# Attention values of two heads made at once with tokens standing, in a fused attention and feed-forward kernel on one core

## The reference

```python
q = (x @ wq).reshape(B, S, 32, 128)
k = (x @ wk).reshape(B, S, 8, 128)
v = (x @ wv).reshape(B, S, 8, 128)
q, k = _rope(q, pos), _rope(k, pos)
allowed = (j <= i) & (j > i - 128)
attn = softmax(where(allowed, q @ k.T * 128**-0.5, neg))
s = (attn @ v).reshape(B, S, 32 * 128) @ wo
g = (silu(xn @ gate) * (xn @ up)) @ down
```

## Time and profile before

| | |
|---|---|
| median of 3 runs (lowest to highest) | 873.48 us (872.38 to 873.61) |
| the profiled execution | 873.48 us |
| its span on the core | 871.0 us |
| mean granted TensorE clock | 0.999 of full |
| instructions | 14447 |
| HBM read, written | 63.41 MB, 8.39 MB |

### The profile page before, as it was taken

One profiled execution on the slowest core, in us unless ns is written; L12 is line 12 of the kernel. 1 busy time (PEld: TensorE's weight loads), 2 busy tenths in 40 slices (PEclk: granted clock), 3 DMA queues, 4 the chain that ended last, 5 costly groups with the idle time before them and its releaser, 6 DMA issues.

```text
span 871.0 us, 14447 instructions
## 1 busy us (share of the span) xinstructions
PE 861.2 (99%) x4340; PEld 725.6 (83%) x4340; DVE 674.5 (77%) x1264; ACT 493.5 (57%) x1322; POOL 577.2 (66%) x500
## 2 busy tenths in 40 slices
PE   8999999999999999999999999999999999999997
PEld 7888888888888888888888888888888888888886
DVE  8877777877686877877776877778665888989876
ACT  5766565655656566656556555665564444444443
POOL 4665566666675776667666757764446887888865
PEclk9999999999999999999999999999999999999999
DMA  8111110131003012100311020116374564655542
GB/s 263 38 49 37 36 39 25 26 97 36 25 14 106 24 36 90 30 24 24 96 36 36 24 85 24 36 48 159 85 212 120 144 179 132 177 150 167 161 133 96
DMA packets 94851, 72.25 MB, mean 83 GB/s; under 512 B 4192, under 2 KB 80480, under 8 KB 94816
## 3 DMA queue, kind: packets, MB, share of 16 engines
q1 hardware_dynamic: 94096, 70.70, 27.6%
q10 hardware_dynamic: 720, 1.11, 0.4%
HBM read 63.41 MB, written 8.39 MB: 82 GB/s over the span
## 4 chain that ended last, share of the span: by engine, by line
PE 91%; DVE 5%; ACT 2%; DMA 1%; POOL 1%; issue 1%; SPq 0%; DVEq 0%
PE ps L38 29%; PE ps L39 29%; PE ps L40 29%; PE ps L1099 3%; PE ps L1079 1%; ACT probs L1242 1%; DMA work<-L_attn_wv 1%; DVE ps L1507 1%; DMA y<-L_attn_x 0%; DVE work L1503 0%; DVE work L1502 0%; DVE work L1509 0%; POOL w_lo L983 0%; POOL pt_lo L1373 0%; DVE xt_lo L1471 0%
## 5 line engine op out<-in xcount | busy, mean ns | idle before, releaser
L38 PE MATMUL ps<-xt_hi,w_lo 128*128 128x512 f32 x412 | 164.5, 399 | 0.4 <-POOL w_lo L209 0.4
L39 PE MATMUL ps<-xt_lo,w_hi 128*128 128x512 f32 x412 | 161.5, 392 | 0.0
L40 PE MATMUL ps<-xt_hi,w_hi 128*128 128x512 f32 x412 | 160.7, 390 | 0.0
L1373 POOL TENSOR_TENSOR pt_lo<-kept,pt_hi 128x512 fp32r<-128x512 f32 x112 | 142.8, 1293 | 24.9 <-ACT pt_hi L1253 24.6
L1368 POOL TENSOR_TENSOR q_lo<-work,q_hi 128x512 fp32r<-128x512 f32 x63 | 81.3, 1292 | 90.9 <-ACT q_hi L1225 90.9
L1242 ACT ACTIVATE probs<-ps,neg_max 128x128 f32<-128x128 f32 x256 | 90.7, 366 | 42.8 <-DVE neg_max L1527 42.8
L1253 ACT ACTIVATE pt_hi<-kept 128x512 fp32r<-128x512 f32 x112 | 69.2, 633 | 65.6 <-DVE kept L1540 65.6
L38 PE MATMUL ps<-wo_hi,o_lo 128*128 (+1 forms) x256 | 99.8, 390 | 0.1
L40 PE MATMUL ps<-wo_hi,o_hi 128*128 (+1 forms) x256 | 99.6, 389 | 0.0
L39 PE MATMUL ps<-wo_lo,o_hi 128*128 (+1 forms) x256 | 99.6, 389 | 0.0
L40 PEld LDWEIGHTS ps<-xt_hi,w_hi 128*128 128x128 f32 x412 | 77.5, 188 | 17.4
(11 more groups left out here) (174 smaller groups left out, 2234.7 us busy)
## 6 DMA issues: line engine op xcount, KB each, us to landing
work<-L_attn_wq SPq DMA_DIRECT2D x32, 256.0 KB, 2.8
work<-L_attn_wo SPq DMA_DIRECT2D x32, 256.0 KB, 2.7
work<-L_ffn_gate_w SPq DMA_DIRECT2D x14, 256.0 KB, 3.7
work<-L_ffn_gate_z SPq DMA_DIRECT2D x14, 256.0 KB, 4.6
work<-L_ffn_gate_s SPq DMA_DIRECT2D x14, 256.0 KB, 5.8
work<-L_ffn_up_w SPq DMA_DIRECT2D x14, 256.0 KB, 2.9
work<-L_ffn_up_z SPq DMA_DIRECT2D x14, 256.0 KB, 4.0
work<-L_ffn_up_s SPq DMA_DIRECT2D x14, 256.0 KB, 4.5
```

The source lines that it names most:

```text
L38: pe.matmul(out, stat[1], mov[0], start=first, stop=False, skip_group_check=grown)
L39: pe.matmul(out, stat[0], mov[1], start=False, stop=False, skip_group_check=grown)
L40: return pe.matmul(out, stat[0], mov[0], start=False, stop=last, skip_group_check=grown)
L1373: pool.tensor_tensor(pt_lo[:, w, :], kept[:, w, :], pt_hi[:, w, :].bitcast(F32), ALU.subtract).then_inc(pt_split, 1)
```

## The change

Values are made for two heads at once, in the heads with even number (par = 0): the transposed input of 128 tokens stands and the value weights of heads g and g + 1 (256 columns) move. A product (piece 5 or 6) makes two of a batch's four token tiles, 2 x 4 k x 3 = 24 matmuls; the result has tokens on the partitions. v_t, `drain_v`, `turn_v` and their semaphore go, and `hi_of_v` and `lo_of_v` work on half the tokens of two heads each. The heads are issued in pairs: 0 and 1, a loop over pairs (2, 3) and (4, 5), then 6 and 7. An even head has 11 weight pieces, an odd one 9, so `SPLIT_AT` has a table for each. While a unit (g, b) is worked off, seven products are made ahead if par equals b (`with_values`), two of them values; otherwise five are made, and of the last query (`HALVED = 4`) k = 0, 1 are made behind j = 1 and k = 2, 3 at j = 2.

```diff
         def over_heads(eng, body):
-            body(0, False)
-            with eng.Fori(1, NKV - 1) as g:
-                body(g, False)
-            body(NKV - 1, True)
+            for g in range(2):
+                body(g, g, False)
+            with eng.Fori(1, NKV // 2 - 1) as pair:
+                body(pair * 2, 0, False)
+                body(pair * 2 + 1, 1, False)
+            body(NKV - 2, 0, False)
+            body(NKV - 1, 1, True)
...
+        SPLIT_AT = (
+            {(0, 0): (0,), (0, 1): (1, 2), (0, 2): (3,), (0, 3): (4, 5), (1, 0): (6,), (1, 1): (7, 8), (1, 2): (9,), (1, 3): (10,)},
+            {(0, 0): (0,), (0, 1): (1,), (0, 2): (2,), (0, 3): (3, 4), (1, 1): (5,), (1, 2): (6, 7), (1, 3): (8,)})
...
+        HALVED = 4
+
+        def with_values(par, b):
+
+            return par == b
+
+        def before(g, par, b, j):
+            if first_unit(g, b):
+                return (2, 4, 5)[j]
+            return (1, 3, 5)[j] if with_values(par, b) else (1, 3, HALVED)[j]
+
+        def after(g, par, b, j):
+            if first_unit(g, b):
+                return (3, None, 6)[j]
+            return (2, 4, 6)[j] if with_values(par, b) else (2, HALVED, None)[j]
+
+        def left(g, par, b, j):
+
+            if first_unit(g, b):
+                return (1, 3, None)[j]
+            return (None, 2, 4)[j] if with_values(par, b) else (None, 2, None)[j]
...
+                if k >= V_:
+
+                    for t in range(2):
+                        tile = slice(b * SEQ + (2 * (k - V_) + t) * P, b * SEQ + (2 * (k - V_) + t + 1) * P)
+                        for c in ks:
+                            last = three_passes(pe, out[:, t * 2 * P:(t + 1) * 2 * P], (xt_hi[:, c, tile], xt_lo[:, c, tile]),
+                                                [values_weights(w)[:, c, :] for w in (w_hi, w_lo)], c == 0, c == KT - 1)
...
                         turn_probs(n)
-                        if ahead and j == QB - 1:
-                            turn_v(un, bn)
                         if j < QB - 1:
                             scores(n + 1, unit, b, j + 1)
                         elif ahead:
                             scores(n + 1, un, bn, 0)
                         if ahead and j < QB - 1:
-                            project(gn, un, bn, before(g, b, j))
+                            first = before(g, par, b, j)
+
+                            project(gn, pn, bn, first, range(2, KT) if j == 2 and first == HALVED else range(KT))
...
-                        if ahead and j < QB - 1 and after(g, b, j):
-                            project(gn, un, bn, after(g, b, j))
+                        if ahead and j < QB - 1 and after(g, par, b, j):
+                            second = after(g, par, b, j)
+                            project(gn, pn, bn, second, range(2) if j == 1 and second == HALVED and not with_values(par, b) else range(KT))
```

On DVE (ACT and POOL in the same way, with the high and low part of the row) the step's middle becomes:

```diff
-                        if ahead and j < QB - 1 and left(g, b, j):
-                            rope(un, bn, left(g, b, j), n + 1 if early else None)
-                        if ahead and j == QB - 1:
-                            lo_of_v(un, bn)
+                        if ahead and j < QB - 1 and left(g, par, b, j):
+                            rope(gn, pn, bn, left(g, par, b, j), n + 1 if early else None)
+                        if ahead and j == QB - 1 and with_values(par, b):
+                            lo_of_v(gn, bn, 1)
                         if more and not early:
                             invert(n + 1)
-                        if ahead and j < 2:
-                            rope(un, bn, before(g, b, j))
-                        if ahead and j == 2:
-                            drain_v(un, bn)
+                        if ahead and roped_beside(g, par, b, j):
+                            rope(gn, pn, bn, before(g, par, b, j))
+                        if ahead and j == 2 and with_values(par, b):
+                            lo_of_v(gn, bn, 0)
```

More of the change, by code:

```diff
@@ L255, in step @@
     def step(self, pool, g, k):
-        x = lambda part, row, hf: self.tokens(part, g, row, hf)
+        whole = lambda row, hf: (self.tokens(0, g, row, hf), self.tokens(1, g, row, hf), ALU.add)
         t1, t2, t3, t4 = (self.row(i) for i in range(4))
-        first, second = self.more[:, 0, :, :], self.more[:, 1, :, :]
         to, a, b, op, needs = (
[L262 to L271, removed]
+            (t1, *whole(0, 1), None),
+            (t2, *whole(0, 0), None),
+            (t1, t1, t2, ALU.subtract, 2),
+            (t3, *whole(1, 1), None),
+            (t4, *whole(0, 1), None),
+            (t3, t3, t4, ALU.subtract, 5),
+            (t2, *whole(1, 1), None),
+            (t2, t2, t1, ALU.subtract, 7),
+            (t4, *whole(1, 0), None),
+            (t4, t4, t2, ALU.subtract, 9))[k]
         if needs is not None:
-            pool.wait_ge(self.sh.sum_step, g * self.STEPS + (needs - self.STEPS))
+            pool.wait_ge(self.sh.sum_step, g * self.STEPS + (needs - 2 * self.STEPS))
         pool.tensor_tensor(to, a, b, op).then_inc(self.sh.sum_step, 1)
@@ L521, in add_gate2 @@
         wait(dve, self.seven_silu, 2 * blk - 1)
-        dve.tensor_tensor(self.gate2[:, :], self.bank(self.C), self.copies[:, 2, :], ALU.add).then_inc(self.added, 1)
+        dve.tensor_tensor(self.copies[:, 2, :], self.bank(self.C), self.copies[:, 2, :], ALU.add).then_inc(self.added, 1)
     def add_up2(self, dve, blk):
@@ L530, in silu_gate2 @@
         wait(act, self.seven_mid, 2 * blk)
-        act.activation(self.sh.tables[:, 1, :], self.gate2[:, :], ACT.Silu).then_inc(self.seven_silu, 1)
+        act.activation(self.sh.tables[:, 1, :], self.copies[:, 2, :], ACT.Silu).then_inc(self.seven_silu, 1)
     def silu_gate1(self, act, blk):
@@ L699, in high_parts @@
                 wait(act, gated, TT - 4 + i)
[L700 removed]
+                act.activation(gate_of(TT - 1 + i)[:, half], acc(TT - 1, half), ACT.Silu).then_inc(gate_done, 1)
         def low_parts(pool):
@@ L1337, in body @@
                         behind = first_unit(g, b) and j == 1
-                        if ahead and j < 2 and not behind:
-                            hi_of_roped(un, bn, before(g, b, j))
+                        if ahead and roped_beside(g, par, b, j) and not behind:
+                            hi_of_roped(gn, pn, bn, before(g, par, b, j))
+                        if ahead and j == 2 and with_values(par, b):
+                            hi_of_v(gn, bn, 0)
                         if not last and j == QB - 1:
-                            hi_of_roped(unit + 2, b, 0)
+                            hi_of_roped(g + 1, 1 - par, b, 0)
                         if last:
```

352 lines of the change are left out of this document (175 added, 177 removed).

## The result

The changed kernel takes 892.15 us (median of 4 runs, 891.08 to 892.41) against 873.53 before: a ratio of 1.0218 with a 95% interval of 1.0205 to 1.0231. The forecast was 887.2 us, its range 881 to 893. Direction and range held; the sum is 5 us short, and the missing part has one main cause, a fall of TensorE's granted clock that the sum had left out.

A forecast was written before the change was run, and what follows sets the result against it. TensorE was taken as the bound, busy 99% of the span with 91% of the chain. Terms -7.0 + 2.1 + 20.0 - 0.5 - 0.9 = +13.7 on 873.5 gave 887.2 us, range 881 to 893.

The forecast's parts named there:

- Removed work, -7.0: TensorE, all 16 units: the four transposes of v_t go, 0.44 us a unit, 7.0 us less.
- Added matmuls, +2.1: TensorE value products: 384 matmuls of 256 columns at 0.119 us for 192 of 512 at 0.227, +2.1 us.
- The wait: TensorE before the scores at j = 3 waits for row 4's low part: 2.5 us in 8 five-product units, +20.0.
- the 0.2 for a late DVE: Part of each wait: lost cover in the step before makes DVE late by up to 0.27 us, 0.2 taken.
- Other covers at nothing: Other steps of five- and seven-product units: cover still holds, no further TensorE wait opens, costed at 0.
- a sign of being wrong: Profile after: the forecast is wrong if TensorE's idle time in the loop ends by something other than POOL q_lo.
- The ends, -0.5 and -0.9: First unit's extra product beyond the sum: -0.5 us (-1 to +2); last head's shorter waits: -0.9 (-1.2 to 0).
- The clock: TensorE's granted clock: full in the forecast; the rival, chance 0.05, loses 2.4 us at each of eight waits, 906 us.
- Rival 2: Second wait, at the weighing of j = 2 for pt_lo: up to 1.3 us in 4 units, 892 us, chance 0.12.
- Rival 1: No wait before the scores at j = 3, row 4's low part being ready: 867.2 us, chance 0.13.

The follow-up runs named there:

- Run 8: Kernel before without the values' four transposes and the copy into v_t (wrong attention values), first feed-forward product's wait kept as before: 869.20 us, ratio 0.9953.
- Run 7: Kernel before with each value product issued as 24 matmuls of 256 columns instead of 12 of 512: 874.38 us, ratio 1.0016.
- Run 9: Kernel before with row 4's rotation at j = 2 behind the reciprocal in every unit but the first, products whole: 878.51 us, ratio 1.0062.
- run 5: The kernel of run 3 with six matmuls of row 0's product moved ahead of the late scores in seven five-product units: 867.13 us, ratio 0.9932.
- run 10: The changed kernel measured once more, with nothing changed: 890.85 us, ratio 1.0203.
- run 3: Changed kernel with the halved row 4 rotated earlier, the reciprocal amid the rotation, ACT normalising before the row's high part: 873.88 us, ratio 1.0011.
- run 4: Changed kernel without halving: row 4 whole behind j = 1, rotated ahead of the reciprocal, no product at j = 2 of five-product units: 885.3 us, ratio 1.0143.

## Why the prediction was right, and where it was short

**Removed work, -7.0:** this was right. Run 8 measured 0.42 to 0.43 us a unit alone, and 0.44 had been taken.

**Added matmuls, +2.1:** this was somewhat too much as a whole. Run 7 measured +1.4 (0.6 to 2.2); the step of 0.119 us itself was right.

**The wait:** the mechanism, its place, its number (eight) and its parts were right. The chain from maxima to low part was 6.66 us for 6.68. The wait was 2.21 to 2.53 us and 18.3 in sum, for 20.0 forecast (first scores matmul less the step's start and 0.35). What failed in size is the 0.2 for a late DVE: its unfold began at 264.69, 0.76 us into the step at 263.93, for 0.64 before, but the row maxima ended at 267.04, 3.11 us into it for 3.10 before, so the lateness did not reach the chain. TensorE started 0.05 us behind the low part, or 0.14 in four of the units, where 0.1 was taken. The longest wait, 2.53, is the first: there the chain took 6.88 us.

The parts of the wait can be told apart with one more line of the kernel before:

```profile
300.72 1.29 POOL L1368 TENSOR_TENSOR q_lo<-work,q_hi 128x512 fp32r<-128x512 f32 x1 [0.60 <-ACT q_hi L1225]
```

There the low part of row 4 was ready at 302.01 and the scores began at 303.42, 1.4 us later. In the changed kernel the low part ends 1.7 us later in the step (9.77 us after its start for 8.03), which is the order, and TensorE could come 1.8 us earlier (7.60 for 9.44), which is the half product and the turning: 1.7 + 1.8 - 1.4 = 2.1 us. Run 9 shows what the order does alone (0.45 a unit, behind whole products), and run 5 that with the rotation earlier and the rest covered nothing is left of the wait.

**Other covers at nothing:** this was mostly right. The turns at j = 2 and j = 3 never waited. But once in the loop a step of 10.65 took 11.56: TensorE waited for pt_lo, which came late behind a pause of DVE that is put down to "issue" (both lines from the changed kernel):

```profile
371.00 0.50 PE L38 MATMUL ps<-pt_hi,v_lo 128*128 128x512 f32 x1 [0.53 <-POOL pt_lo L1420]
...
368.24 0.69 DVE L1584 TENSOR_TENSOR kept<-ps,keep_sb 128x512 f32<-128x512 f32 x1 [2.33 <-issue]
```

The forecast named such a wait, idle time in the loop that ends by something else than q_lo, as a sign of being wrong; it cost 0.9 us. It falls at the seam of the loop's two iterations, of which each now holds two heads, and all runs from the changed kernel have it there (0.9 to 1.7 us); the kernel before has no such step at its seams. That the jump back over a body twice as long causes it was not tried.

**The ends, -0.5 and -0.9:** the last unit's steps lost 1.2 us. At the start the first probabilities are turned at 40.18 us for 38.36, 1.8 later, where one product more without the turning would be 2.6 (2.86, and 0.14 for the other value product, less 0.44): 0.7 gained, where 0.5 was forecast. The "883 to 892" of these terms is narrower than they are: all low ends together give 881.8, all high ends 894.2.

**The clock:** this is the step that failed. The forecast held the granted clock at full in its own case, a term of nothing, and gave the fall a chance of 0.05 as a rival, because no stretch before had a wait of 2.5 us between work. It came in 5 of 8 waits (4 in run 10), 1.60 us each and 8.0 in all. The rival put the price at 2.4 for each, read off the idle products at the start, and at all eight waits, which made its 906 us too high. The Trainium skill (TensorE: Matmul & The Clock Gate, on the HAM clock gate) says idleness throttles the array; the trace agrees, with 0.50 granted from 110 to 113 us.

**Rival 2**, a second wait for pt_lo at the weighing of j = 2, did not occur; its allowance up to 893 is what let the range hold the time. So the range held by luck, by a price that belonged to something else, and with 0.9 us to spare. **Rival 1** is refuted by the eight waits. Its sum without them, -6.3 us, is near what run 5 measured, -5.8 with one wait of 0.8 and the seam's 0.9 left in it.

The steps now add up, from the span of 871.0: start +4.5 up to the second unit (two value products more than before lie in it), fourteen units without waits 545.5 for 556.4, or -10.9, the last unit -1.2, waits +18.3, clock +8.0, seam +0.9: +19.6, as measured (890.6). The units came out near the forecast where the clock held: 42.2 us with seven products for 42.3, and 38.7 to 38.8 with five for 39.

## What to carry to other kernels

Work that only fills an engine's time is cover for a chain on the others. Before a product is moved, halved or dropped, write down for that step both the time at which the busy engine will arrive and the end of the chain it will then meet, with every instruction now queued ahead of the one that ends last. A rotation that was free beside the exponentials cost 0.45 us a unit behind the reciprocal with the cover whole, and 2.2 with half a product and the turning gone as well. Where a wait of 1 to 2 us is forecast on TensorE, price the clock too: the time at half rate added 44% to these waits. Once the waits were covered, the same idea was worth 5.8 us.

## What was not expected of the hardware

- A TensorE idle time of 2.2 to 2.5 us, in a stream that is otherwise without a gap, let the granted clock fall to half in 5 of 8 cases in one execution and 4 of 8 in another, three of them the same; in the case shown the fall came 1.2 us after TensorE had resumed work. Waits of up to 1.2 us (run 3) and of mostly 0.45 us (run 9) left the mean at 0.999. But in run 4 a wait of 1.0 us, followed at once by four turns that took 1.07 us for 0.35, let it fall in 2 of 8 cases.
- With weight loads between, float32r matmuls step by 0.227 us at 512 columns and 0.120 at 256: by these steps a matmul cut in two costs 13 ns. By the time of run 7, where 192 were cut, it is 7 ns each (3 to 12).
